# Two adaLN blocks on one core: the second layer's convolution by pairs of heads with a placing transfer, and its MLP's output bias as a row added by GpSimd

## The reference

```
h   = layernorm(x) * (1 + ca) + sa
avg = cumsum(h, tokens) / (1, 2, 3, ...)            # [1024, 256] = 16 heads of 16 features
pc  = avg_head @ W_pe + b_pe                        # per token and head: 31 dynamic, 31 gate
w   = softmax(energy + sigmoid(gate) * dynamic)     # 31 weights per token and head
conv[t, head, :] = sum_k w[t, head, k] * avg[t + k - 30, head, :]
v   = layernorm(conv @ W_fc.T + h) * gamma + beta
x   = x + ga * v
h   = layernorm(x) * (1 + cb) + sb
x   = x + gb * (relu(h @ W1 + b1) @ W2 + b2)
```

## Time and profile before

| what | value |
|---|---|
| timed runs | 3459.31, 3462.36, 3465.0 us; median 3462.36 |
| profiled execution, own time | 3466.14 us |
| its span, first to last instruction | 3464.3 us |
| mean granted clock of TensorE | 0.979 of 2.4 GHz |
| busy in the span | PE 3307.4, PEld 2785.4, DVE 2606.8, ACT 2076.2, POOL 1269.7 us |
| same, as shares | PE 95%, PEld 80%, DVE 75%, ACT 60%, POOL 37% |

### The profile page before, as it was taken

One profiled execution on the slowest core, in us unless ns is written; L12 is line 12 of the kernel. 1 busy time (PEld: TensorE's weight loads), 2 busy tenths in 40 slices (PEclk: granted clock), 3 DMA queues, 4 the chain that ended last, 5 costly groups with the idle time before them and its releaser, 6 DMA issues.

```text
span 3464.3 us, 67597 instructions
## 1 busy us (share of the span) xinstructions
PE 3307.4 (95%) x25168; PEld 2785.4 (80%) x25168; DVE 2606.8 (75%) x6172; ACT 2076.2 (60%) x4055; POOL 1269.7 (37%) x1073
## 2 busy tenths in 40 slices
PE   7999999999996999999999469999999999999999
PEld 4888888888885799999999347888888888888888
DVE  5877887788777865555554578888888888888884
ACT  4677777777765555655665345555555555555554
POOL 1333333332331366666665332333333332322320
PEclk8999999999998999999999689999999999999999
DMA  5332233222212344444444465555655555655541
GB/s 180 102 114 90 93 114 108 80 64 80 75 45 80 87 115 103 96 104 109 105 97 86 86 132 113 113 127 127 129 125 127 120 123 126 130 125 128 128 102 41
DMA packets 746021, 366.38 MB, mean 106 GB/s; under 512 B 551278, under 2 KB 696246, under 8 KB 745558
## 3 DMA queue, kind: packets, MB, share of 16 engines
q1 hardware_dynamic: 717278, 319.57, 36.4%
q0 software_dynamic: 28416, 42.49, 6.6%
HBM read 224.93 MB, written 135.99 MB: 104 GB/s over the span
## 4 chain that ended last, share of the span: by engine, by line
PE 87%; DVE 6%; ACT 2%; DMA 2%; issue 1%; SPq 1%; POOL 1%; POOLq 0%; DVEq 0%; ACTq 0%
PE bank L2294 10%; PE bank L853 10%; PE bank L1612 10%; PE bank L2308 10%; PE bank L1596 10%; PE bank L833 10%; PE bank L2265 7%; PE bank L130 5%; PE bank L810 3%; PE bank L2244 3%; PE bank L2276 3%; PE bank L2239 1%; ACT sides L1140 1%; PE bank L818 1%; PE bank L846 1%
## 5 line engine op out<-in xcount | busy, mean ns | idle before, releaser
L1492 DVE TENSOR_TENSOR hidden_low<-bank,hidden_high 128x512 fp32r<-128x512 f32 x256 | 176.2, 689 | 263.0 <-ACT hidden_high L1193 262.8
L609 ACT ACTIVATE bank<-bank,b 128x512 f32<-128x512 f32 x256 | 172.7, 675 | 282.2 <-PE bank L833 281.9
L1186 ACT ACTIVATE bank<-bank,fc_bias 128x512 f32<-128x512 f32 x256 | 169.5, 662 | 263.5 <-PE bank L1596 263.5
L853 PE MATMUL bank<-w_high,gT_low 128*128 128x256 f32 x1024 | 309.8, 303 | 2.9 <-DVE gT_low L725 2.9
L2052 ACT ACTIVATE bank<-bank,l_b 128x512 f32<-128x512 f32 x256 | 168.9, 660 | 238.8 <-PE bank L2294 238.8
L2308 PE MATMUL bank<-l_w_high,l_hidden_low 128*128 128x256 f32 x1024 | 307.6, 300 | 0.0
L2265 PE MATMUL bank<-bandT,window 128*32 128x96 f32 x5632 | 271.2, 345 | 22.4 <-DMA bandT<-bands 20.2
L853 PE MATMUL bank<-w_low,gT_high 128*128 128x256 f32 x1024 | 289.4, 283 | 0.0
L853 PE MATMUL bank<-w_high,gT_high 128*128 128x256 f32 x1024 | 289.4, 283 | 0.0
L2308 PE MATMUL bank<-l_w_low,l_hidden_high 128*128 128x256 f32 x1024 | 286.0, 279 | 0.0
L2308 PE MATMUL bank<-l_w_high,l_hidden_high 128*128 128x256 f32 x1024 | 285.5, 279 | 0.0
(11 more groups left out here) (372 smaller groups left out, 10709.3 us busy)
## 6 DMA issues: line engine op xcount, KB each, us to landing
bandT<-bands SPq DMA_DIRECT2D x352, 240.0 KB, 3.7
fc_full<-in_L_ffn_fc_wT SPq DMA_DIRECT2D x32, 1024.0 KB, 5.5
bands<-zeros SPq DMA_DIRECT2D x22, 768.0 KB, 8.6
x<-in_L_attn_x SPq DMA_DIRECT2D x32, 512.0 KB, 6.3
moe_output<-zeros SPq DMA_DIRECT2D x32, 512.0 KB, 7.1
x_after_retention<-x SPq DMA_DIRECT2D x32, 512.0 KB, 2.9
moe_input_and_gates<-xn SPq DMA_DIRECT2D x32, 512.0 KB, 7.7
moe<-moe_output SPq DMA_DIRECT2D x32, 512.0 KB, 7.4
```

Of the source, the lines that this page charges most:

```text
L609: e.activation(bank[:, :], bank[:, :], ACT.Gelu_apprx_tanh, bias=t.b1[:, f:f + 1]).then_inc(s("g_full"), 1)
L853: m = pe.matmul(out, x, w, start=False, stop=f == KF - 1 and j == 2 and c % 2 == 1)
L1492: v.tensor_tensor(t.hidden.low[:, n % SLICES, :], K.banks[t.bank["expand", i, f, 0]][:, :], t.hidden.high[:, n % SLICES, :], ALU.subtract) ...
```

## The change

The convolution. `window` loses its zero columns: it is 32 columns wide for a pair, the two heads' features interleaved (feature 0 of the even head, feature 0 of the odd head, and so on). The moving operand is both heads' columns at once, 96 tokens x 2 neighbouring values. A pair is one matmul of 192 columns; a tile has 8, and none accumulates. The result holds each head's rows times both heads' bands; even output rows are right in the even columns, odd rows in the odd columns. ACT copies the odd columns to a new tile `odd_heads`, then the even columns of all rows to `convT`, and a transfer issued by ACT (`place_odd`, 64 partitions x 2 x 96 values) puts the odd rows of `odd_heads` over the odd rows of `convT`. `mix` now waits for that transfer. W_fc's rows are permuted on the host to match.

The bias. The two L2304 matmuls for each half go, with the `out_bias` tile and its preparation. `make_rows` makes a fifth row gb * b2 in layer zero; `load_last_row` (SP) brings it in once for each batch, and a new GpSimd step `add_last` adds it to x2, 128 x 1024, after `norm_x3` has read x2 and before `result`, which now also waits for it.

All places and hold times of layer one are written anew. The core of the diff:

```diff
@@ PLACES_D
...
+    "load_band": (13.87, 15.88, 16.4, 18.65, 19.95, 21.42, 22.38, 24.27, 25.46, 27.03, 29.11), "load_gain_row": 17.56,
+    "convolve": (16.98, 18.08, 19.68, 21.04, 22.23, 23.96, 25.03, 26.91, 28.63, 29.74, 31.19),
+    "place_odd": (17.09, 18.19, 19.9, 21.15, 22.42, 24.02, 25.25, 27.02, 28.74, 29.85, 31.3),
+    "mix": (19.14, 20.6, 22.09, 24.88, 26.54, 27.89, 31.18, 32.34),
+    "add_last": (31.21, 37.87), "load_last_row": 24.08, "turn_mid": (30.56, 37.64), "load_out_row": 34.73,
...
@@ make_rows
+        v.tensor_tensor(rows[:, 4, :], field(K, t0, 1, 5), t0.vec[:, 4, :], ALU.mult)
@@ layer_one_tiles
-    t.window = K.ring(ctx, "window", 2, [P, H // 2, 2, 2 * t.HD])
+    t.window = K.ring(ctx, "window", 2, [P, H // 2, 2 * t.HD])
+    t.odd = K.ring(ctx, "odd_heads", 2, [P, KD, TT])
@@ layer_one_pool
+        elif name == "add_last":
...
+            e.wait_ge(s("h4"), n + 1)
+            e.wait_ge(*K.later("row_last", 16 * (b + 1)))
+            e.tensor_tensor(x2[:, :, :], x2[:, :, :], t.row_last[:, :].unsqueeze(1).to_broadcast([P, HC, D]), ALU.add).then_inc(K.later("x_last")[0], 1)
@@ layer_one_scalar
         elif name == "convolve":
             (i,) = args
             n, size, place = b * NT + i, min(TT, K.S - i * TT), i * TT % t.CIRCLE
             e.wait_ge(s("conv_product"), n + 1)
             before = C * b + ((i - 4) * TT + TT - 1) // P + 1 if i >= 4 else C * b
+            if n >= 2:
+                e.wait_ge(*K.later(f"odd_placed{n % 2}", 16 * (n // 2)))
+            heads = K.banks[t.bank["convolve", b, i, 0]][:, 0:2 * KD * TT].rearrange("p (k t q) -> p k t q", k=KD, q=2)
+            e.copy(t.odd[n % 2][:, :, 0:size], heads[:, :, 0:size, 1])
             if before:
                 e.wait_ge(s("mixed"), before)
-            e.copy(t.convT[:, :, place:place + size],
-                   K.banks[t.bank["convolve", b, i, 0]][:, 0:KD * TT].rearrange("p (k t) -> p k t", k=KD)[:, :, 0:size]).then_inc(s("convT"), 1)
+            e.copy(t.convT[:, :, place:place + size], heads[:, :, 0:size, 0]).then_inc(s("conv_taken"), 1)
+        elif name == "place_odd":
...
+            e.wait_ge(s("conv_taken"), n + 1)
+            e.dma_start(t.convT[1::2, :, place:place + size], t.odd[n % 2][1::2, :, 0:size]).then_inc(K.later(f"odd_placed{n % 2}")[0], 16)
@@ layer_one_vector
         elif name == "result":
             n = 2 * b + args[0]
             v.wait_ge(s("o_gain"), n + 1)
+            v.wait_ge(*K.later("x_last", n + 1))
@@ layer_one_tensor
             for k in range(KD):
-                for odd in range(2):
-                    for g in range(4):
-                        pair = 4 * k + g
-                        m = pe.matmul(bank[32 * g:32 * (g + 1), k * TT:(k + 1) * TT], t.window[n % 2][:, pair, odd, :],
-                                      t.bandT[n % 2][:, :, g // 2 * H // 2 + k * t.HR + g % 2 * 2 + odd], start=odd == 0, stop=odd == 1)
+                for g in range(4):
+                    first = g // 2 * H // 2 + k * t.HR + g % 2 * 2
+                    out = bank[32 * g:32 * (g + 1), 2 * k * TT:2 * (k + 1) * TT].rearrange("p (t q) -> p t q", q=2)
+                    m = pe.matmul(out, t.window[n % 2][:, 4 * k + g, :], t.bandT[n % 2][:, :, first:first + 2], start=True, stop=True)
@@ mix
-            pe.wait_ge(s("convT"), NT * b + -(-(ch + 1) * P // TT))
+            last = NT * b + -(-(ch + 1) * P // TT) - 1
+            for n in range(max(last - 1, 0), last + 1):
+                pe.wait_ge(*K.later(f"odd_placed{n % 2}", 16 * (n // 2 + 1)))
@@ l1_contract
-            if f == 0:
-                for pair in range(2):
-                    bank = take(6 + pair, "o_gain", n + 1)
-                    pe.matmul(bank[:, :], t.ones[:, :], t.out_bias[:, :, :].rearrange("o a d -> o (a d)"), start=True, stop=False)
```

More of the change, by code:

```diff
@@ L220, in conditioning_tiles @@
     t.work = K.tile(ctx, "mod_work", [K.B, 4, K.D])
-    t.vec = K.tile(ctx, "vectors_by_batch", [K.B, 4, K.D])
-    t.rows = [K.tile(ctx, "rows0", [K.B, 4, K.D]), K.tile(ctx, "rows1", [K.B, 4, K.D])]
+    t.vec = K.tile(ctx, "vectors_by_batch", [K.B, 5, K.D])
+    t.rows = [K.tile(ctx, "rows0", [K.B, 4, K.D]), K.tile(ctx, "rows1", [K.B, 5, K.D])]
     t.mod = K.ring(ctx, "mod", 2, [K.B, K.NM])
@@ L294, in make_rows @@
     v.wait_ge(K.dve_step, c.n)
[L295 removed]
+    v.wait_ge(s("vectors"), 80)
     rows = t0.rows[n]
@@ L1642 @@
-    "mix": (19.06, 20.4, 21.9, 24.8, 26.2, 27.7, 30.6, 31.43), "center_mid": (19, 20.4, 21.9, 24.8, 26.21, 27.7, 30.6, 32),
-    "root_mid": (24.98, 32.56), "residual_mid": (25.83, 32.44), "stats_x3": (26.59, 34.51), "root_x3": (27.13, 35.02), "norm_x3": (27.48, 35.68),
-    "turn_mid": (29.71, 36.62), "load_out_row": 35.09, "gain_out": (42.68, 50.91), "result": (45.63, 54.65),
+    "l1_split": 0.57, "l1_low": 1.11, "l1_contract": 2.54, "share": (2.62, 10.23), "load": (0.24, 7.43),
+    "join": (4.53, 13.01), "add_in": (5.06, 13.03), "stats_in": (6.81, 13.73), "root_in": (8.43, 14.8),
@@ L1739, in layer_one_tiles @@
     t.hidden = K.split_tile(ctx, "l1_hidden", [P, SLICES_D, BANK])
-    t.row_gain, t.row_bias, t.row_out = (K.tile(ctx, n, [P, D]) for n in ("row_gain", "row_bias", "row_out"))
+    t.row_gain, t.row_bias, t.row_out, t.row_last = (K.tile(ctx, n, [P, D]) for n in ("row_gain", "row_bias", "row_out", "row_last"))
     t.h3T, t.avgT = K.ring(ctx, "h3T", 2, [P, KD, S]), K.ring(ctx, "avgT", 2, [P, KD, PAD + S + PAD])
```

147 lines of the change are left out of this document (78 added, 69 removed).

## The result

The changed kernel is slower: 3524.58 us (median of 4 runs, 3517.49 to 3535.05) against 3461.57 (4 runs), ratio 1.0184 with a 95% interval of 1.0156 to 1.0211. The prediction said 3358. The profiled execution took 3525.55 us, its span is 3523.7. In what follows a batch's time is the distance between the same step of TensorE in successive batches, as a mean over 12 batches: 89.96 us before, 94.15 now; the forecast was 83.5.

The account below looks back on a forecast made before the run. TensorE's queue was taken as the bound: 81.8 us of its own + 1.1 of transfer stalls + 0.6 for VectorE = 83.5 us a batch, 104 us less over 16 batches, giving 3358 us; range 3332 to 3450.

Parts of the forecast that it names:

- What bounds the kernel before, and the convolution's price: TensorE's queue sets the 89.98 us batch; halving the convolution's step saves 0.65 us a tile, 7.1 us a batch.
- the gaps: Convolution's moving operand: values 64 bytes apart hold it at half its speed at full clock; with neighbours the step halves.
- the rival on delivery: Convolution: four streams reading the same partitions are limited in sum, so it stays at 1.46 us; total 3450 to 3462 us; chance 0.16.
- A microsecond taken from it there is a microsecond, until VectorE, 12 us behind, takes over.: TensorE's queue in layer one: time taken from it shortens the batch fully, until VectorE's 77.9 us of work bounds it.
- VectorE takes over: Convolution halves but 6 of VectorE's 12 us of waits stay; batch 85.1 us, total time 3384 us; chance 0.19.
- The order: VectorE's waits, 6.3 us a batch for GpSimd's energies, mostly go in the new order; 0.6 us a batch is added.
- The placing transfer: Between convolution and mix: landing 2.7 us, chain 3.55 us (2.95 to 5.05), stalling TensorE 1.1 us a batch.
- The rival on the slower side: At the matmuls behind each mix, placing-transfer stalls eat the 8.2 us gain; 3548 us at 5 us landing; chance 0.07.
- add_last: GpSimd's two 2.41 us steps a batch are hidden; their collisions cost VectorE 1.2 us, bounds 0 and 2 x 1.5.
- The bias matmuls': Removing TensorE's two bias pairs, 0.53 us each, saves 1.1 us a batch, 17 us in all.

Follow-up runs that it names:

- the first run: The kernel before, with each convolution matmul reading 96 neighbouring values of bandT instead of values 64 bytes apart: ratio 0.9945, 3446.08 us, batch 88.84 us.

## Why the prediction was wrong, point by point

*What bounds the kernel before, and the convolution's price.* Right: TensorE's queue set the batch, the gaps were the cause, and 16 matmuls took what they should, at both clocks. So the rival on delivery is out.

*"A microsecond taken from it there is a microsecond, until VectorE, 12 us behind, takes over."* This is the step that failed. VectorE's work was 12 us behind, but its loop with GpSimd and ScalarE closed at 88.8 us, 1.1 behind (the first run, and again with pairs and no transfer in the order of the kernel before). I had read the earlier trace rows, 6.3 us a batch of waits for GpSimd's energies, as slack that an order would remove. They were part of a loop: shortening GpSimd's step brought 84.64 us, and no placing that was run did. The forecast without the transfer's stalls was 81.8 + 0.6 = 82.4; 88.75 is 6.35 above it, the largest part of the miss (that run has the bias on TensorE still, which the forecast hadn't). The rival *VectorE takes over* named the mechanism, at 85.1 too low a price, since it let VectorE lose half of its waits.

*The order.* The prediction took the new order for one that closes VectorE's waits. It did so for GpSimd's energies, but VectorE's work grew by 3.5 us. Without the transfer it costs 2.0 us: 88.75 in the old, 90.75 in the new. A later mix is what the transfer asks for; VectorE then waits for mix's product once a batch, 2.3 us without transfer and addition.

*The placing transfer.* 3.4 us a batch in the new order where 1.1 stood. What TensorE has to do between a convolution and its mix was counted well: 3.3 us at chunk 1, 3.2 at chunk 5, 5.7 at chunk 4, for 3.0, 3.0 and "5 or more". The chain was not: 2.6 + 5.8 = 8.4 us for tile 6, where 3.55 stood and 5.05 was the bound. The landing was taken as one number, 2.7; it is 1.9 to 7.2, and it depends on the tile, by what SP issued before. The issue was taken as 0.85 us behind the convolution; it is 0.65 for most tiles, but 2.6 for tile 6. The earlier trace rows had the sign of it: L1877 landed after 2.1 to 11.4 us, of which I used the shortest and a middle. The sum, 82.4 + 6.35 + 2.0 + 3.4, is 94.15. It is one way through the runs, by differences: the parts act on each other, and taken in the old order the transfer alone would be 13.8.

*The rival on the slower side* had the right place but not the amount: the 3.4 us alone would have left a gain on the forecast's other terms. That the run is slower, as this rival has it, came from the loop as much.

*add_last.* Its collisions were put at 1.2 us, at most 3.0; alone in the old order they cost 3.0, and in the new one, without the transfer, 3.3 us of VectorE's busy time (84.4 against 81.1) and nothing of the batch (90.73 and 90.76). In the earlier trace rows VectorE's instruction doesn't end when the other has, but 0.53 us later. (The Trainium skill, SBUF — State Buffer, Who interferes with whom, has GpSimd or VectorE hold the shared ports for a whole instruction. The four instructions above agree, two of which ended 0.28 us after one of GpSimd's.)

*The bias matmuls'* 1.1 us have their price in the earlier trace rows, but no run shows them come back: with the bias alone TensorE is busy 89.4 us a batch, before 89.5, and the batch is 1.9 longer. That they are worth nothing where the loop is last is argued from this, not shown by a run of its own.

## What to carry to other kernels

Before counting a microsecond of the busiest engine as a microsecond, price the loop of the others: work that two engines hand to and fro, waits included, is their time, not their slack; an experiment that only makes the busiest engine faster, on any data, shows that bound in one run. Price a transfer in a chain between engines tile by tile, by what other queues have just issued (here 1.9 to 7.2 us); fewer bytes in the same number of pieces didn't help. And an instruction moved to an idle GpSimd can be paid by VectorE: here 4.8 us of it a batch cost VectorE 3.0 to 3.3. Last, count what the profile counts: an fp32 matmul of this kernel is two of its instructions.
